# A branch's two forms change places, and the constants' transfers become steps of the timeline

## What is computed

```python
h = _silu(_tlin(x, w1_w, w1_s)) * _tlin(x, w2_w, w2_s)     # 256 -> 1024
h = gelu(_tlin(h, h1_w, h1_s))                             # 1024 -> 1024
h = gelu(_tlin(h, h2_w, h2_s))                             # 1024 -> 1024
return _tlin(h, w3_w, w3_s)                                # 1024 -> 256
...
scores = einsum(q, k_g) * scale + pos_bias; attn = softmax(scores)
out = (einsum(attn, v_g) * sigmoid(x @ Wgate + bgate)) @ Wout + bout
...
x = x + 0.5 * ffn(layernorm(x))
x = x + attention(layernorm(x))
x = x + 0.5 * ffn(layernorm(x))
```

## Time and profile before

| | |
|---|---|
| median of 3 runs | 1610.91 us (1610.43 to 1613.33) |
| profiled execution | 1609.98 us, of which span 1608.1 us |
| PE / PEld busy | 1528.4 (95%) / 1224.9 (76%) |
| DVE / ACT / POOL busy | 1086.0 (68%) / 677.6 (42%) / 553.3 (34%) |
| mean granted clock of PE | 0.987 of full |
| chain that ended last | PE 66%, DVE 12%, POOL 8%, DMA 7%, ACT 4%, issue 3% |

### The profile page before, as it was taken

One profiled execution on the slowest core, in us unless ns is written; L12 is line 12 of the kernel. 1 busy time (PEld: TensorE's weight loads), 2 busy tenths in 40 slices (PEclk: granted clock), 3 DMA queues, 4 the chain that ended last, 5 costly groups with the idle time before them and its releaser, 6 DMA issues.

```text
span 1608.1 us, 19160 instructions
## 1 busy us (share of the span) xinstructions
PE 1528.4 (95%) x6978; PEld 1224.9 (76%) x6978; DVE 1086.0 (68%) x1475; ACT 677.6 (42%) x1062; POOL 553.3 (34%) x402
## 2 busy tenths in 40 slices
PE   7689999999999999999999999999999999998998
PEld 6567888777777778787777877768788877786887
DVE  6323758894777686777876877778675978793322
ACT  7434445344343435344534353434343444352442
POOL 2003051535171607162526070533614245434020
PEclk9899999999999999999999999999999999999999
DMA  7662848666766494857765757557474776754332
GB/s 308 252 241 101 281 140 302 224 207 226 232 234 218 155 312 142 279 171 262 261 229 183 251 182 261 185 192 254 157 265 158 269 247 223 269 198 157 118 100 71
DMA packets 189218, 342.41 MB, mean 213 GB/s; under 512 B 15552, under 2 KB 138560, under 8 KB 188736
## 3 DMA queue, kind: packets, MB, share of 16 engines
q1 hardware_dynamic: 189120, 341.13, 62.1%
HBM read 319.05 MB, written 30.41 MB: 217 GB/s over the span
## 4 chain that ended last, share of the span: by engine, by line
PE 66%; DVE 12%; POOL 8%; DMA 7%; ACT 4%; issue 3%; SPq 0%; DVEq 0%; POOLq 0%; ACTq 0%
PE f_bank L1101 22%; PE f_bank L1102 22%; PE a_banks L1179 6%; PE f_bank L1030 4%; PE f_bank L1031 4%; DMA weights_hi<-in_ffn_w 3%; POOL acc L693 3%; PE f_bank L1130 2%; PE f_bank L1131 2%; DVE slot L935 2%; DVE slot L979 2%; DVE S L941 2%; POOL acc L690 2%; PE a_banks L1199 1%; POOL h_lo L707 1%
## 5 line engine op out<-in xcount | busy, mean ns | idle before, releaser
L1101 PE MATMUL f_bank<-h_hi,wring 128*128 128x512 f32 x2048 | 824.4, 403 | 31.1 <-POOL h_lo L707 12.4
L1102 PE MATMUL f_bank<-h_lo,wring 128*128 128x512 f32 x2048 | 813.6, 397 | 0.0
L1101 PEld LDWEIGHTS f_bank<-h_hi,wring 128*128 128x128 f32 x2048 | 387.6, 189 | 131.9 <-issue 18.4
L1102 PEld LDWEIGHTS f_bank<-h_lo,wring 128*128 128x128 f32 x2048 | 387.6, 189 | 93.2 <-issue 1.4
L773 ACT ACTIVATE h_hi<-f_bank,colv 128x512 fp32r<-128x512 f32 x256 | 176.5, 689 | 553.1 <-PE f_bank L1102 552.9
L895 DVE TENSOR_TENSOR h_lo<-f_bank,h_hi 128x512 fp32r<-128x512 f32 x256 | 175.2, 687 | 258.5 <-ACT f_bank L774 256.8
L707 POOL TENSOR_TENSOR h_lo<-f_gated,h_hi 128x512 fp32r<-128x512 f32 x128 | 165.4, 1305 | 449.1 <-ACT h_hi L767 448.3
L1030 PE MATMUL f_bank<-fT_hi,w_in 128*128 128x512 f32 x480 | 197.5, 411 | 11.6 <-ACT f_gated L762 5.4
L1031 PE MATMUL f_bank<-fT_lo,w_in 128*128 128x512 f32 x480 | 191.5, 399 | 0.0
L979 DVE TENSOR_TENSOR slot<-slot,a_banks 128x1280 f32<-128x1280 f32 (+4 forms) x124 | 169.5, 1375 | 21.1 <-DMA slot<-keys_and_values 20.7
L935 DVE TENSOR_TENSOR slot<-slot,a_banks 128x1280 f32<-128x1280 f32 (+4 forms) x124 | 170.5, 1375 | 17.0 <-DMA slot<-keys_and_values 16.8
(11 more groups left out here) (117 smaller groups left out, 1328.1 us busy)
## 6 DMA issues: line engine op xcount, KB each, us to landing
wring<-weights_hi SPq DMA_DIRECT2D x256, 512.0 KB, 4.6
slot<-keys_and_values SPq DMA_DIRECT2D x128, 384.0 KB, 4.9
slot<-keys_and_values SPq DMA_DIRECT2D x64, 640.0 KB, 4.0
slot<-keys_and_values SPq DMA_DIRECT2D x312, 128.0 KB, 4.4
slot<-keys_and_values SPq DMA_DIRECT2D x64, 256.0 KB, 5.7
weights_hi<-in_ffn_w SPq DMA_DIRECT2D x16, 512.0 KB, 5.0
keys_and_values<-kv_out SPq DMA_DIRECT2D x32, 256.0 KB, 2.3
xf<-in_x SPq DMA_DIRECT2D x8, 512.0 KB, 5.8
```

The source lines that it names most:

```text
L1101: pe.matmul(bank[:, :], hi, h_hi[src][:, k, :], start=(k == 0), stop=False)
L1102: last = pe.matmul(bank[:, :], hi, h_lo[src][:, k, :], start=False, stop=(not general and k == KH - 1))
```

## The change

- On SP and PE the condition is turned round, so that the short form is written first and the general one in `Else`. On SP the wait for the zeros ahead of the branch is gone.
- SP's transfers of `rowv` and `wo` become the step `w_rows` (planned time 0.5), those of `wproj` and the zeros the step `w_proj` (5.0), both in the timeline behind the branch.
- DVE's wait for the constants and its three scalings become the step `w_scale` (17.0). `w_max`, `w_log` and `w_merge` move from 2.0, 3.0 and 6.0 to 18.0, 20.0 and 24.0.
- The waits for zeros and constants move to their first users: SP's first load of keys, POOL's first `a_bout` and first `a_add`.

```diff
-            steps += [(2.0, "w_max", ()), (3.0, "w_log", ()), (6.0, "w_merge", ())]
+            steps += [(0.5, "w_rows", ()), (5.0, "w_proj", ()), (17.0, "w_scale", ()), (18.0, "w_max", ()),
+                      (20.0, "w_log", ()), (24.0, "w_merge", ())]
...
-            sp.dma_start(rowv[:, :], rows.partition_broadcast(P)).then_inc(s_const, 16)
-            sp.dma_start(wo[:, :, :], out_w).then_inc(s_const, 16)
-
-            sp.wait_ge(s_compared, BLOCKS - 1)
-            sp.dma_start(wproj[:, :, :], proj_w).then_inc(s_const, 16)
-            sp.wait_ge(s_zero, 1)
-            sp.dma_start(kv_dram[:, :, 0:PAD, :].rearrange("t b p d -> p (t b) d"),
-                         acc[:, 0:1, :].to_broadcast([P, 2 * B, D])).then_inc(s_padded, 16)
             sp.wait_ge(s_flag, 1)
             has_lo = sp.value_load(flag[0:1, 0:1])
...
+            def w_rows():
+                sp.dma_start(rowv[:, :], rows.partition_broadcast(P)).then_inc(s_const, 16)
+                sp.dma_start(wo[:, :, :], out_w).then_inc(s_const, 16)
+
+            def w_proj():
+
+                sp.wait_ge(s_compared, BLOCKS - 1)
+                sp.dma_start(wproj[:, :, :], proj_w).then_inc(s_const, 16)
+                sp.wait_ge(s_zero, 1)
+                sp.dma_start(kv_dram[:, :, 0:PAD, :].rearrange("t b p d -> p (t b) d"),
+                             acc[:, 0:1, :].to_broadcast([P, 2 * B, D])).then_inc(s_padded, 16)
...
             def a_k_load(a, n, g):
+                if (a.i, n, g) == (0, 0, 0):
+                    wait_alone(s_padded, 16)
...
-            sp.wait_ge(s_padded, 16)
-            with sp.If(has_lo != 0):
+            with sp.If(has_lo == 0):
+                run(False)
+            with sp.Else():
                 lo_parts()
                 run(True)
-            with sp.Else():
-                run(False)
...
             def a_bout_(a):
                 rows_ = xa[:, a.u, :, :]
+                if a.i == 0:
+                    pool.wait_ge(s_const, 16 * 3)
...
                 if g == 1:
+                    if (a.i, n) == (0, 0):
+                        pool.wait_ge(s_padded, 16)
...
-            pool.wait_ge(s_padded, 16)
-            pool.wait_ge(s_const, 16 * 3)
...
+            def w_scale():
+                dve.wait_ge(s_const, 16 * 3)
+                dve.tensor_scalar(s3, s3, 0.5, None, ALU.mult).then_inc(s_scaled, 1)
+                dve.tensor_scalar(q_bias, q_bias, SCALE, None, ALU.mult).then_inc(s_scaled, 1)
+
+                dve.tensor_scalar(wo[:, :, :], wo[:, :, :], 0.5, None, ALU.mult).then_inc(s_scaled, 1)
+                dve.wait_ge(s_scaled, 3)
...
-            dve.wait_ge(s_const, 16 * 3)
-            dve.tensor_scalar(s3, s3, 0.5, None, ALU.mult).then_inc(s_scaled, 1)
-            dve.tensor_scalar(q_bias, q_bias, SCALE, None, ALU.mult).then_inc(s_scaled, 1)
-
-            dve.tensor_scalar(wo[:, :, :], wo[:, :, :], 0.5, None, ALU.mult).then_inc(s_scaled, 1)
-            dve.wait_ge(s_scaled, 3)
...
-            with pe.If(has_lo != 0):
+            with pe.If(has_lo == 0):
+                run(False)
+            with pe.Else():
                 run(True)
-            with pe.Else():
-                run(False)
```

More of the change, by code:

```diff
@@ L643, in run @@
                     "f_load": f_load_, "f_store": f_store, "a_load": a_load, "a_store": a_store,
-                    "a_kv_store": a_kv_store, "a_k_load": a_k_load, "a_v_load": a_v_load, "fill": fill, **({} if general else {"copy": copy}),
+                    "a_kv_store": a_kv_store, "a_k_load": a_k_load, "a_v_load": a_v_load, "fill": fill,
+                    "w_rows": w_rows, "w_proj": w_proj, **({} if general else {"copy": copy}),
                 }, [*timeline()[0], *ring.fills()])
-            sp.wait_ge(s_padded, 16)
-            with sp.If(has_lo != 0):
+            with sp.If(has_lo == 0):
+                run(False)
+            with sp.Else():
                 lo_parts()
                 run(True)
-            with sp.Else():
-                run(False)
             for p in range(2):
@@ L991, in a_residual @@
                                   ALU.add).then_inc(a_x, 1)
-            dve.wait_ge(s_const, 16 * 3)
-            dve.tensor_scalar(s3, s3, 0.5, None, ALU.mult).then_inc(s_scaled, 1)
-            dve.tensor_scalar(q_bias, q_bias, SCALE, None, ALU.mult).then_inc(s_scaled, 1)
-            dve.tensor_scalar(wo[:, :, :], wo[:, :, :], 0.5, None, ALU.mult).then_inc(s_scaled, 1)
-            dve.wait_ge(s_scaled, 3)
-            schedule({"w_max": w_max, "w_merge": w_merge, "f_stats": f_stats_, "f_tlo": f_tlo_, "f_gate": f_gate, "f_lo": f_lo_,
+            schedule({"w_scale": w_scale, "w_max": w_max, "w_merge": w_merge, "f_stats": f_stats_, "f_tlo": f_tlo_, "f_gate": f_gate, "f_lo": f_lo_,
                       "f_residual": f_residual, "a_stats": a_stats_, "a_evict": a_evict, "a_score": a_score,
```

## The result

The changed kernel took 1602.72 us (median of 6 runs, 1599.92 to 1604.65), the kernel before 1612.89 us in the same comparison (6 runs, 1610.43 to 1613.48). The ratio is 0.9947, 95% interval 0.9935 to 0.9959: against the 1610.91 that the forecast started from this is 8.5 us faster, between 6.6 and 10.5. (The two medians themselves lie 10.2 us apart, inside that interval; the text goes by the ratios.) The forecast was 1603.5, 7.4 us faster. The profiled execution was the slowest of the six, 1604.65, with a span of 1602.9, 5.2 us shorter than the span before.

The account below looks back on a forecast made before the run. It took SP's chain of copies to bound PE's first pass: 7.7 - 0.3 = 7.4 us off the span, 1608.1 to 1600.7; the profiled execution then 1602.6, the median 0.9 above, 1603.5; range 1599.0 to 1608.5.

Parts of the forecast that it names:

- What bounds the first pass: First pass: PE follows SP's chain of copies, 5.4 us a block where PE needs 3.7; its start outweighs PE's own.
- The branch: Branch on PE and SP: flag reading and falling through take 1.5 us, bounds 0 and 4.6; both go on near 52.0.
- Rival B: Branch: as dear wherever its target lies; gain 5 us, 1605.9, or 2.5 us, 1608.4, if SP pays 7.2; chance 0.15.
- When copy 6 lands: SP's queue in the first pass: behind the constants' load copy 6 lands at 71.0, 7.7 us earlier; ends 4.6 and 11.5.
- Rival A: SP's queue in the first pass: the load doesn't delay copy 6; gain 11.2 us, 1599.7; chance 0.10.
- From copy 6 to the end of the pass: First pass, blocks 6 to 15: the chain's shift of 7.7 us arrives at the pass's end.
- The chain rules as before: First pass from block 8 on: SP's chain sets the pace as before, 5.4 us a block.
- Steps moved on other engines: ACT and DVE: w_log makes the sixth gelu 1.9 us late; w_scale and w_max fit idle time; no cost.
- The exit: End of kernel: PE and SP jump over the long form; SP's costs nothing at 2.45 us, 4.7 at 7.2; taken 0.3.
- Rival C: End of kernel: the exit jump costs its full loaded price, 4.7 us; gain 3.0 us, 1607.9; chance 0.08.
- Rival D: PE's clock, blocks 6 to 15: new waits keep it at 1.2 GHz, slower, 1614.5; decides below 0.69; chance 0.04.
- The sum: Whole kernel: 7.7 us from the first pass less 0.3 at the exit, 7.4 us off the span.

Follow-up runs that it names:

- experiment 1: The kernel before with only the order of the two forms turned round, short form first; 0.9978 to the kernel before, 3.5 us faster.
- experiment 7: The changed kernel with copies 24 instead of 14 ahead of use: 0.9869 to the kernel before with constants late, 0.9917 with constants where the change put them.
- experiment 3: The kernel before without its general form, short form still in Else, so the taken jump goes to near code; 0.9972 to the kernel before.
- experiment 2: The changed kernel with the two branches as before, so only steps and waits are changed; 0.9974 to the kernel before, 4.2 us faster.
- experiment 8: The changed kernel with copies 24 ahead, constants late and the long form first again; 0.9923 to the kernel before.
- experiment 5: The changed kernel with the constants' transfers behind the first pass's last fill, and the scalings and merges late; 0.9924 to the kernel before.
- experiment 6: The changed kernel with only the scalings, w_max, w_log and w_merge late, transfers unchanged; 0.9957 to the kernel before.

## Why the prediction was right, point by point

**What bounds the first pass.** Right. PE follows SP's chain of copies: a start 6.6 us earlier moved block 15 by 1.0 us (experiment 1), and taking the chain apart took PE's waits for weights away (experiment 7).

**The branch.** The reading of the flag with a branch that falls through was put at 1.5 us, between 0 and 4.6; it costs PE 0.85 and SP 0.64 (49.75 to 50.39). Rival B, the branch as dear wherever its target lies, is refuted by experiments 1 and 3. That the difference between 7.0 and 2.45 us was load is supported by experiments 2 and 8, 4.66 and 4.3 us without the constants; that is still more than SP's 2.45, and this remainder isn't explained.

**When copy 6 lands.** Forecast 71.0, measured 69.9; 0.65 to 0.9 us of the shift is the branch, 0.76 the earlier opening; counted from the flag it is 20.5 forecast and 20.2 measured, so the rest of the term was 0.3 to 0.6 us too short. The 1 us to the first packet and the 1.3 us of tail stood in the sum without a row; copy 4 of the kernel before, issued at 66.35, moved its first packets between 67.5 and 68.0, and no run shows the tail by itself. The load in front of it was well sized: 3.8 us between the forecast and its lower end, 3.5 measured in experiment 5. Rival A, that the load doesn't delay copy 6, is refuted by the same run.

**From copy 6 to the end of the pass.** Block 15 was forecast at about 119 and came at 119.55. Two errors cancel here, and that is luck: in the second profile of the same kernel it came at 122.45. The chain started 1 us earlier than forecast and was slower: from fill 6 to the last fill 45.6 us (69.99 to 115.59) where the kernel before took 44.1 (78.73 to 122.85). "The chain rules as before" was the weakest step of the argument: the ten traces of the kernels with this chain in the first pass give between 43.3 and 48.2 us for these nine blocks, since each copy's landing varies between 4 and 7 us and each of them counts in full.

**Steps moved on other engines.** Right, no cost (experiment 6).

**The exit.** Mis-sized: taken as 0.3 us of a range from 0 to 4.7, it costs 1.3. The step that failed is "at 2.45 us it costs nothing". SP's jump took more than 3.3 us at the exit, not 2.45, and so outlasts the landing, though that has itself become slower, from 2.9 to 3.7 us; why it takes longer there stays open. Rival C had the right mechanism at a third of its price.

**The clock.** Rival D didn't come. Where PE waited for blocks 6 to 15, it was granted 0.91 on average from 80 to 100 us and 1.00 in the windows on both sides; the average is far from the point of 0.69. The low clock isn't absent, though: from 90 to 95 us it was 0.66, behind waits of 1.06 and 2.76 us, and eight matmuls stood 0.43 us apart instead of 0.23, some 1.5 us in all. It cost little here: PE still waited 0.78 us for weights behind it (101.25), and would have waited longer. In experiment 1 such a stretch fell behind the last wait and counted in full.

**The sum.** 7.4 us forecast, 8.5 (6.6 to 10.5) measured. The first trace accounts for 7.1 at the first pass's end, 0.76 of it from the opening, less 1.3 at the exit: 5 to 6 us. That this first store agrees with the forecast's shift of 7.7 is in part luck: over the five traces with the changed kernel's order of transfers the first store's lead goes from 4.2 to 9.2 us, 6.9 on average. What the times have beyond it isn't traced with certainty; the traces do show leads that come and go in passes that the change doesn't touch. Windows of the kernel before and of the changed one (length, busy of PE, PEld, DVE, ACT, POOL, PE clock, DMA share, GB/s):

```profile
926.00:1130.00 204.00, 193.25 (x867) 153.32 (x866) 151.43 (x192) 85.78 (x135) 84.70 (x58) 0.97 0.64 213
435.00:630.00 195.00, 188.31 (x861) 150.30 (x860) 148.24 (x198) 82.59 (x132) 85.87 (x58) 0.99 0.65 217
```

```profile
926.00:1130.00 204.00, 192.56 (x881) 152.36 (x879) 154.25 (x199) 85.46 (x135) 92.03 (x62) 1.00 0.65 217
435.00:630.00 195.00, 186.74 (x848) 149.15 (x848) 143.54 (x194) 80.25 (x129) 84.51 (x58) 0.98 0.63 212
```

The first pair is before, the second after. Between 926 and 1130 the kernel before had a lower clock and lost 3.8 us to the changed one (the lead at the stores there grows from 4.0 to 7.8); around 435 to 530 the changed kernel lost 3 us. Against the kernel before, nearly every trace gains 2 to 4 us between the stores of 926 and 1130, the branch order alone 2.2. So part of each difference to this one profile of before belongs to that profile. Why the branch order alone and the last experiment moved the medians by more than their first passes did stays open; no second profile of the kernel before was taken.

## What to carry to other kernels

A fully unrolled form that is not taken should not lie between a branch and the form that is: put the likely form first, and count the jump at the exit, which then lies beside the last store only as far as that lasts. Where an engine's queue alternates a transfer and a wait for its landing, the latency of each landing is paid in full, and an earlier start of the consumer hardly helps (1.0 us of 6.6 in experiment 1); issue the transfers two or three steps ahead of their waits. Move bulk transfers whose users come much later behind such a chain, not to its head: here this was worth 3.5 us at fill 6, and with the copies ahead as well the first store came 10.4 us earlier than in the changed kernel (132.62 and 122.19).

## What the runs showed of the hardware

One and the same far jump cost PE 7.0 us with 3.3 MB of transfers in flight behind the flag, 4.66 and 4.3 us with less (a mean DMA share of 0.94 in the first gap, 0.37 and 0.40 in the others), and 0.97 us once its target was near. A branch that falls through and the reading of a flag from SBUF cost 0.85 us together on PE. The far jump of SP cost 2.45 us in the middle of the kernel, about 3.3 us behind the flag in experiment 2 (3.9 less the 0.64 of the changed kernel), and over 3.3 us at the exit, where its packets moved 2.5 and 4.5 us behind the store's issue. PE's jump was slower with the constants' load beside it, and its jump at the exit goes with a store that lands 0.6 to 1.5 us later; that instruction fetch and data hinder each other is the likely reading of both, not tried apart. Copies of 512 KB from DRAM to DRAM, one under way at a time beside a fill, mostly landed 4.2 to 5.3 us after their issue (up to 7.0, in experiment 2), and 8.75 us with the constants in front. With 3.3 MB of constants and four copies issued ahead of it, the issue of a further copy held SP's queue for 7.11 us (experiment 7). PE was granted 0.51 of its clock from 91.3 to 94.7 us in the changed kernel, its lower level, and eight matmuls took 1.5 us longer for it.
